# Mamba block and soft decision tree on one core: tail weights scaled in two parts, path matrices and statistics moved, warming products left out

## What is computed

```python
mod = silu(c) @ wmod                            # sa, ca, ga, sb, cb, gb
ga, gb = (2 * (g >= 0) - 1) * maximum(abs(g), 0.25)      # for both gates
h = layernorm(x) * (1 + ca) + sa
xp, z = split(h @ W_in)                         # 256 channels each
u = silu(causal_conv4(xp) + conv_b)
dt_r, B, C = split(u @ W_xp)                    # 8, 16, 16
delta = softplus(dt_r @ W_dt + dt_bias)
for t: s = exp(delta_t * A) * s + delta_t * B_t * u_t     # state 256 x 16
       y_t = s . C_t + D_skip * u_t
x = x + ga * ((y * silu(z)) @ W_out)
h = layernorm(x) * (1 + cb) + sb
gate = sigmoid((h @ Wq.T) @ routers.T)          # 255 nodes of a tree
prob = product of gate or 1 - gate along each of 256 paths
x = x + gb * ((prob @ leaf_values) @ Wo.T + Wo_b)
```

## Time and profile before

| | us |
|---|---|
| median of 3 runs | 511.05 |
| lowest, highest run | 510.07, 511.46 |
| profiled execution, its own time | 512.9 |
| its span, first to last instruction | 510.9 |
| busy: DVE, POOL, PE, ACT | 460.8, 427.0, 407.7, 368.4 |

### The profile page before, as it was taken

How to read it: one execution, slowest core, us unless ns; L and a number is a source line. 1 busy time by engine, 2 the same in 40 slices (tenths; PEclk the granted TensorE clock), 3 DMA queues, 4 the chain that set the end, 5 groups by cost and what they waited for, 6 DMA issues and landing times. The chain is left out here.

```text
span 510.9 us, 6652 instructions
## 1 busy us (share of the span) xinstructions
PE 407.7 (80%) x2111; PEld 283.5 (55%) x2143; DVE 460.8 (90%) x550; ACT 368.4 (72%) x673; POOL 427.0 (84%) x238
## 2 busy tenths in 40 slices
PE   8979652797679967997979787996789786666787
PEld 5437331575556745584647555673547554554554
DVE  5889694899999999999999999998899989999961
ACT  2378972378876998588967998698766896448654
POOL 2549788999999889998899899989799889989700
PEclk9999885799779988898989988999889997796999
DMA  7484033220262008300453008300722027300001
GB/s 176 135 276 163 1 105 147 103 83 1 89 268 83 1 6 308 125 23 1 147 208 104 1 25 330 104 2 0 261 95 103 1 65 291 103 2 1 21 1 41
DMA packets 23714, 51.06 MB, mean 100 GB/s; under 512 B 4473, under 2 KB 13824, under 8 KB 19584
## 3 DMA queue, kind: packets, MB, share of 16 engines
q1 hardware_dynamic: 23680, 50.64, 28.9%
HBM read 48.01 MB, written 2.62 MB: 99 GB/s over the span
## 5 line engine op out<-in xcount | busy, mean ns | idle before, releaser
L568 POOL TENSOR_TENSOR hc<-h,c_rows 128x1024 f32<-128x1024 f32 x126 | 296.0, 2363 | 30.8 <-DVE h L1291 24.0
L1291 DVE TENSOR_TENSOR_SCAN h<-dA,state,dbu 128x512 f32<-128x512 f32 x192 | 233.4, 1264 | 3.8 <-ACT dA L656 3.8
L656 ACT ACTIVATE dA<-delta,a_neg 128x512 f32<-128x512 f32 x256 | 173.9, 686 | 55.7 <-DVE h L1291 54.9
L1070 PE MATMUL yb<-ident,hc 128*128 128x128 f32 x1024 | 162.4, 295 | 26.6 <-POOL hc L568 24.2
L1070 PEld LDWEIGHTS yb<-ident,hc 128*128 128x128 f32 x1024 | 136.9, 154 | 77.4 <-issue 49.3
L1304 DVE TENSOR_TENSOR dbu<-du,bb 128x1024 f32<-128x1024 f32 x88 | 105.5, 1199 | 7.6 <-PE bb L1095 2.6
L555 POOL TENSOR_TENSOR dbu<-du,b_rows 128x1024 f32<-128x1024 f32 x40 | 94.5, 2363 | 4.3 <-DMA b_rows<-bc_dram 4.3
L1291 DVE TENSOR_TENSOR_SCAN h<-dA,dbu 128x512 f32<-128x512 f32 x64 | 74.1, 1204 | 10.0 <-POOL dbu L555 6.6
L1095 PE MATMUL bb<-b_parts,sel 128*128 128x512 bf16 x63 | 27.3, 433 | 45.1 <-DVE dbu L1304 44.3
L976 PE MATMUL mf<-f_hT,w_conv 128*128 128x512 f32 x112 | 53.4, 601 | 1.8 <-ACT zu L715 1.2
L1095 PEld LDWEIGHTS bb<-b_parts,sel 128*128 128x128 bf16 x88 | 9.0, 102 | 63.3 <-DVE dbu L1304 34.5
(11 more groups left out here) (200 smaller groups left out, 529.1 us busy)
## 6 DMA issues: line engine op xcount, KB each, us to landing
c_rows<-bc_dram SPq DMA_DIRECT2D x32, 1024.0 KB, 7.4
b_rows<-bc_dram SPq DMA_DIRECT2D x40, 256.0 KB, 9.0
xs<-in_L_attn_x_dram SPq DMA_DIRECT2D x8, 256.0 KB, 3.8
out_dram<-xs SPq DMA_DIRECT2D x7, 256.0 KB, 5.8
ygT<-in_L_attn_conv_w_dram SPq DMA_DIRECT2D x1, 512.0 KB, 5.0
bc_dram<-xd SPq DMA_DIRECT2D x8, 64.0 KB, 1.6
probT<-in_L_wmod_dram SPq DMA_DIRECT2D x1, 384.0 KB, 3.9
w_in<-in_L_attn_W_in_dram SPq DMA_DIRECT2D x1, 256.0 KB, 4.1
```

Source lines behind the costliest of these rows:

```text
L568: nc.gpsimd.tensor_tensor(hc[:, pair % RC, :, :], h[:, pair % RH, :, :], c_rows[:, q, n % NQ, :].unsqueeze(1).broadcast_to([P, HALVES, T]) ...
L656: nc.scalar.activation(dA[ke % RD][:, :], delta[:, ge % 2, half, :], ACT.Exp, scale=a_neg[:, half, n:n + 1]).then_inc(s_dA, 1)
L1070: last = nc.tensor.matmul(bank[:, tile], hc[:, pair % RC, half, tile], ident[:, :], start=False, stop=n == N - 1, is_transpose=True, skip_ ...
L1291: v.tensor_tensor_scan(h[:, pair % RH, half, :], dA[k % RD][:, :], dbu[:, pair % RW, half, :], start, ALU.mult, ALU.add).then_inc(s_scan, 1)
```

## The change

- **Path matrices.** `make_paths` moves from step 20 of group 0 into POOL's prologue, in three pieces: levels 1 and 2 behind the constants, 3 and 4 behind DVE's normalised x of group 0, 5 to 7 behind the selectors. Each of the three selects of `sel` is cut in two of 1024 columns.
- **Tail weights.** `scale_output_weights` stays at step 20 of group 0; `scale_leaf_weights` runs at step 10 of group 1 and has a semaphore of its own, on which the leaf product of group 0 waits (in group 2).
- **Statistics.** Those of groups 2 and 3 run in DVE's prologue, behind the high and the middle part of B. 1/std and offsets of both groups are made together at steps 2 and 3 of group 0. In the loop, step 19 of group g has the statistics of group g+4, so groups 0 to 3 have one each and group 4 none. The arrays have a place for each group.
- **Gate values.** DVE computes them behind the copy of the dt product weights, no longer ahead of it.
- **Warming.** `keep_warm_on(dA[2], 6)` goes.
- **silu of z.** Step 10 of group g takes z of group g, and runs in group 7 too, with its two table loads.

```diff
-    W_TURN, W_COPY, W_MUL, W_TAKE, W_SCALE = (3, 7), (5, 9), 10, 12, 20
+    NORMS = {2: (4, 3)}
+    NORMS.update({g: (g + 1, g) for g in range(4, GROUPS)})
+    W_TURN, W_COPY, W_MUL, W_TAKE, W_SCALE = (3, 7), (5, 9), 10, 12, (20, 10)
...
+            chain(nc.gpsimd.memset(path[:, :, :], 0.0))
+            chain(nc.gpsimd.memset(path[0:1, 1, :], 1.0))
+            make_paths(1, 3)
+            pool.wait_ge(s_fxh, 1)
+            make_paths(3, 5)
+            pool.wait_ge(s_wconv, TAPS)
...
+            chain(nc.gpsimd.memset(sel[:, :, :], 0.0))
+            for first in (B_HI, B_MID, B_LO):
+                for part in range(2):
+                    some = sel[:, part * N // 2:(part + 1) * N // 2, :]
+                    picked = nc.gpsimd.affine_select(out=some, in_=some, compare_op=ALU.not_equal, fill=1.0,
+                                                     base=-first - part * N // 2, pattern=[[-1, N // 2], [0, P]],
+                                                     channel_multiplier=1)
...
+            make_paths(5, DEPTH)
...
+            def scale_output_weights():
+
                 pool.wait_ge(s_gates, 1)
                 pool.wait_ge(s_w, 16 * n_rest)
...
+            def scale_leaf_weights():
+
+                pool.wait_ge(s_wtake, 1)
...
-                    if g == 0 and s == W_SCALE:
-                        scale_tail_weights()
-                        make_paths()
-                    if 2 <= m2 < GROUPS and s == N_OFF:
-                        offset(m2, f_mv, s_frs, f_nm, s_fnm)
+                    if g == 0 and s == W_SCALE[0]:
+                        scale_output_weights()
+                    if g == 1 and s == W_SCALE[1]:
+                        scale_leaf_weights()
+                    if m2 in NORMS and s == N_OFF:
+                        f_offset(m2, *NORMS[m2])
...
-                        for fz in (0, 1) if f == 1 else (f,):
-                            wait_read(act, "f", "z", 1, fz)
-                            z_part = zu[:, fz % 2, 0:HALVES, :]
-                            nc.scalar.activation(z_part, z_part, ACT.Silu).then_inc(s_zsilu, 1)
+                        wait_read(act, "f", "z", 1, g)
+                        z_part = zu[:, g % 2, 0:HALVES, :]
+                        nc.scalar.activation(z_part, z_part, ACT.Silu).then_inc(s_zsilu, 1)
...
                 gate_products()
-                keep_warm_on(dA[2], 6)
                 pe.wait_ge(s_h0, 1)
...
                         wait_read(pe, "t", "lp", 1, g)
+                        if g == 0:
+                            pe.wait_ge(s_lready, 1)
...
                 gates()
-
                 dve.wait_ge(s_wdtp, 1)
                 v.tensor_copy(w_xdt[:, :, :],
                               dA[0][:, 0:HALVES * DI].rearrange("p (h e) -> p h e", h=HALVES)).then_inc(s_wdt, 1)
+                gate_values()
...
                 v.tensor_copy(b_parts[:, 0, :], mb["f"][0][:, :]).then_inc(s_hi, 1)
+                dve.wait_ge(s_x, 16 * (GROUPS - 2))
+                stats(2, f_bn, f_mv[:, 2, :, :], s_fvar)
                 dve.wait_ge(s_r1, 1)
                 v.tensor_copy(b_parts[B_MID:P, 0, :], mb["f"][0][B_MID:P, :]).then_inc(s_mid, 1)
+                stats(3, f_bn, f_mv[:, 3, :, :], s_fvar)
                 dve.wait_ge(s_r2, 1)
...
-                    if 2 <= g + 3 < GROUPS and s == N_STATS:
-
-                        dve.wait_ge(s_x, 16 * (GROUPS - 2))
-                        if g >= 0:
-                            dve.wait_ge(s_fnm, g + 1)
-                        stats(g + 3, f_bn, f_mv, s_fvar)
+                    if 4 <= g + 4 < GROUPS and s == N_STATS:
+                        stats(g + 4, f_bn, f_mv[:, g + 4, :, :], s_fvar)
```

More of the change, by code:

```diff
@@ L477, in _, with t_offset, f_offset, make_paths @@
             nc.gpsimd.memset(zeros[:, :], 0.0).then_inc(s_const, 1)
[L479 to L503 removed]
+            def t_offset(g):
+                pool.wait_ge(s_trs, g + 1)
+                nc.gpsimd.tensor_tensor(t_nm[:, :], t_mv[:, :, 0], t_nm[:, :], ALU.mult).then_inc(s_tnm, 1)
+            def f_offset(first, end, ready):
+                pool.wait_ge(s_frs, ready)
+                nc.gpsimd.tensor_tensor(f_nm[:, first:end, :], f_mv[:, first:end, :, 0], f_nm[:, first:end, :],
+                                        ALU.mult).then_inc(s_fnm, 1)
+            def make_paths(first, end):
+                for level in range(first, end):
                     nodes = 1 << (level - 1)
@@ new lines, in _ @@
+            chain(nc.gpsimd.memset(sel[:, :, :], 0.0))
[5 more added lines that the diff above has]
+                                                     channel_multiplier=1)
+                    if first == B_LO and part:
+                        picked.then_inc(s_sel, 1)
+                    else:
+                        chain(picked)
@@ L527, in scale_tail_weights @@
+            def scale_leaf_weights():
+                pool.wait_ge(s_wtake, 1)
+                for i in range(2):
+                    chain(nc.gpsimd.tensor_tensor(leaf_out[:, i, :], leaf_out[:, i, :], wo_b[:, :], ALU.add))
+                for b in range(BATCH):
+                    for i in range(2):
                         last = nc.gpsimd.tensor_tensor(leaf_out_g[:, b, i, :], leaf_out[:, i, :], gate_raw[:, b, 1, :],
                                                        ALU.mult)
-                last.then_inc(s_wready, 1)
+                last.then_inc(s_lready, 1)
@@ L586, in chain, with rstd @@
                 act.wait_ge(s_aseq, seq)
-            def rstd(g, mv, rs, nm, ready, done):
-                act.wait_ge(ready, g + 1)
-                chain(nc.scalar.activation(rs[:, :], mv[:, :, 1], ACT.Ln, bias=eps_col[:, :]))
-                chain(nc.scalar.activation(rs[:, :], rs[:, :], ACT.Exp, scale=-0.5))
-                nc.scalar.activation(nm[:, :], rs[:, :], ACT.Copy, scale=-1.0).then_inc(done, 1)
+            def rstd(var, rs, nm, ready, count, done):
+                act.wait_ge(ready, count)
+                chain(nc.scalar.activation(rs, var, ACT.Ln, bias=eps_col[:, :]))
+                chain(nc.scalar.activation(rs, rs, ACT.Exp, scale=-0.5))
+                nc.scalar.activation(nm, rs, ACT.Copy, scale=-1.0).then_inc(done, 1)
             def normalise(g, rs, nm, ready, count, xhat, done):
@@ L1187, in stats @@
             def stats(g, bn, mv, ready):
+                if g:
+                    dve.wait_ge(ready, g)
                 for i in range(TILES):
@@ L1219, in gates, with gate_values @@
                 copy.then_inc(s_gatec, 1)
+            def gate_values():
                 dve.wait_ge(s_gatec, 1)
```

70 lines of the change are left out of this document (27 added, 43 removed).

## The result

| | before | changed |
|---|---|---|
| median of 4 runs each | 511.25 us | 499.09 us |
| lowest, highest run | 510.07, 514.30 | 496.99, 500.31 |
| ratio of the medians, 95% interval | | 0.9755 [0.9717, 0.9793] |
| profiled execution, its span | 512.9, 510.9 | 496.99, 494.8 |
| mean granted clock of PE in it | 0.903 | 0.934 |

The kernel is 12.2 us faster; 498.6 (496.0 to 502.6) was forecast. The profiled execution of the changed kernel is the fastest of its four and that of before was over its median, so the two traces lie 16.1 us apart, 4 more than the medians.

A forecast was written before the change was run, and what follows sets the result against it. DVE, busy 460.8 of 510.9 us, was taken as the bound. Gains of 9.1 + 1.2 + 1.0 + 1.2 = 12.5 us gave 500.4 us for the profiled execution and 498.6 us at the median, range 496.0 to 502.6.

The forecast's parts named there:

- POOL's stop, 9.1 us: Step 20 of group 0: shortening POOL's late work removes DVE's waits of 6.62 and 2.46 us, gain 9.1 us.
- 1.7 costs nothing: Step 20 of group 0: POOL's remaining stop of 1.7 us is under the 2.7 us that buffers absorb, cost 0.
- 2.8 costs nothing: Step 10 of group 1: POOL's new work of 2.8 us is covered by slack, cost 0, bounds 0 and 2.8.
- The rival in which it comes back: Groups 0 and 1: POOL's stops return, 503.1 in full, 500.9 by half; shared chance 0.25 with port and slow clock.
- silu of z, 1.0 us: Step 10 of group 0: one z piece fewer ahead of dA gains 1.0 us; group 7's extra work is covered.
- Warming products, 1.2 us: Prologue, PE: without the filler u products start 2.35 us sooner and end 1.2 us sooner; bounds -1.25 and 2.35.
- if the clock rises at the moment it does now: Prologue, PE: clock rises at 13.9 us, 2.6 of eight records done by then, end at 16.3 instead of 17.5.
- The rival "slower": Into group 0: without the filler the clock stays at 1.2 GHz, PE becomes the bound, 515 and above; chance 0.02.
- The relay behind it: Prologue to first scan: PE's 1.2 us pass on; moving group 2's statistics books nothing more, bounds 0 to 1.2.
- DVE as the prologue's bound: Prologue rival: POOL's selects delay DVE, first part of B 0.9 us later, 500.7; shared chance 0.25 with stops and clock.
- Statistics of group 7, 1.2 us: Group 4 of the loop: DVE has one set of statistics fewer, gain 1.2 us as DVE sets the pace.
- the slack that I forecast from the idle DMA engines: Prologue: x is loaded by 22.4 us, when DMA engines go idle, and DVE reaches the statistics at about 23.6.

The follow-up runs named there:

- e7: Changed kernel with silu of z taken a group ahead again (two pieces at step 10 of group 0, none in group 7): 502.29 us.
- e2: Kernel before without the six warming products, nothing else: 511.68 us, ratio 1.0009 [0.9984, 1.0034].
- e3: Changed kernel with the six warming products back: 498.99 us, ratio 0.9757.
- e6: Changed kernel with statistics where they stood before (group 2's before the first dbu, group g+3's at step 19 of group g): 499.14 us.
- e11: Changed kernel with statistics of group g+3 at step 19 from group 1 on, none in group 0: 498.49 us.
- e12: Changed kernel with selectors made by three whole selects and statistics of group g+3 at step 19 from group 1 on: 498.28 us, ratio 0.9721.
- e9: Changed kernel with leaf weights also scaled at step 20 of group 0, paths still in the prologue: 502.51 us.
- e10: Changed kernel with selectors made by three whole selects of 2048 columns: 498.03 us, ratio 0.9704.
- e1: Kernel before with POOL's part alone (paths in the prologue, selectors halved, tail weights in two parts): 502.19 us, ratio 0.9811.
- e8: Changed kernel with group 4's statistics at step 12 of group 0, groups 5 to 7's at step 19 of groups 2 to 4: 500.27 us.

## Why the prediction came out right

*POOL's stop, 9.1 us.* Right, in size and in mechanism: 8.8 us alone in the runs, both waits gone. The 2.7 us of absorbed stop, read from one row pair, was the number on which "1.7 costs nothing" and "2.8 costs nothing" rested, and stops of three lengths bear it out at 2.4 to 2.7. The rival in which it comes back falls: the buffers absorbed the short stops with DVE running on. One sum of it was off without harm: the last six selects are longer than the mean of 0.49 us of all 14 (3.61 us in the loop and 4.06 in the prologue, not 2.9), and the six half selectors took 7.73 us, not 6.35; so the paths were made at 25.8 us and not at 23.4.

*silu of z, 1.0 us.* Right: 2.81 - 1.86 = 0.95 us between the two kernels, 0.94 in e7, and group 7's hole is covered.

*Warming products, 1.2 us.* Right in direction and mechanism, low in size. The `u` products ended 6.03 us after the start of the gate products instead of 7.84: 1.8 us sooner, where 1.2 were booked within bounds of -1.25 and 2.35. The step that missed is "if the clock rises at the moment it does now", 13.9 us, 4.2 behind the start of the gate products. In the changed kernel's profile the `u` records stand 0.85 and 0.72 us apart at first and 0.43 from 13.22 us on, 3.3 behind that start, so the rise came some 0.9 us sooner. As this moment differs between profiles of the same instructions, the size met here is in part luck. In the runs the gain is not shown: e2's interval allows 0.8 us at most, and e3 equals the changed kernel. The rule of the Trainium skill, "TensorE: Matmul & The Clock Gate", Part 1, that activity itself releases the throttle, agrees with the `u` products: 4.32 us for eight records without the filler, where all at the lower level, 0.85 apart, would have been some 6.8. The rival "slower" falls too: the mean granted clock is 0.934, against 0.903 before.

*The relay behind it.* I booked 0 for the statistics taken out ahead of the first `dbu`, with 0 to 1.2 as bounds, since PE's chain sets the second mark. That was right. The statistics are worth 1.15 us at the first scan (e6), and nothing at the second mark, which follows the end of the `u` records by 25.3 us whether they are moved or not (7.84 and 33.19 before, 6.94 and 32.27 in e3, 6.03 and 31.36 in the changed kernel). The whole 1.8 us at the second mark is the gain of the `u` products.

*DVE as the prologue's bound.* Half true. DVE does run without a gap from 13.51 to the first cast, and there DVE and PE arrive together: PE's product ends at 20.49 + 2.06 = 22.55 and the cast starts at 22.62. In e6 the `u` products end 0.7 us sooner than in the changed kernel, and the first cast still comes 12.7 us after the gate products in both, so there DVE is the bound: a faster PE gains no more at this cast. The two-input operations, which I took as free of POOL, took 1.58 and 1.46 us instead of 0.68 and 0.69. In the changed kernel's profile this costs at most the 0.07 us between 22.55 and 22.62.

*Statistics of group 7, 1.2 us.* **This step failed.** The prediction says that DVE's loop has one fewer, "as DVE sets the pace there". It sets the pace on average, but not at step 19 of group 4: two scans on stands a wait for ACT's `dA`, 0.46 us with the statistics ahead of it and 1.63 without. Group 4 takes 55.34 us instead of 55.51, where 1.2 less was forecast, and e6 has the same time with all statistics at their old places. What is worked off just ahead of a wait is free, and taking it out gained next to nothing. The row with the 0.46 was in the trace of before, in the sum of 7.0 us over 7 waits for `dA`, of which I looked at one only.

So the sum of 12.5 met the measured 12.2 with one term 1.2 too high, one 0.6 too low, and the rest within a few tenths: the terms that traces and runs bear out are 8.8 + 0.95 + 1.8 = 11.6. That the sum came so close is in part luck. The remaining half microsecond is under what the runs can tell. In the two profiles groups 1 to 3 are also 0.3 to 0.5 us shorter each, 1.3 us in all, and the cause stays open. In group 3, 0.41 of the 0.52 us is a wait of DVE for `bb` at 225.87, which the changed kernel's profile lacks. e6, e11 and e12, with the statistics of group g+3 at step 19 as before, have this wait as well, but e7, e9 and e10 have the new steps and a group 3 of 55.8 to 56.0 us, as long as before.

*The low clock.* The two profiles differ by 16.1 us, 4 more than the medians. Before, PE's granted clock is 0.78 and 0.79 from 56 to 64 us, and DVE waits 1.22 us at 62.07 for `bb`; at 363.09 and 365.75 in group 5 it waits 0.57 and 1.44. The changed kernel's profile has nothing at the first two places and 0.42 at the third; its group 5 is 1.3 us shorter. So 1.2 + 1.3 = 2.5 us of the 4 are these. The other profiles speak for episodes and against an effect of the change. A pair of waits for PE, 0.3 to 1.4 and then 1.45 us, stands between 37 and 46 us in those of e1, e2, e6, e7, e9 and e12 and in none of the other eight, with filler and without, with either place of the statistics and of z; e8 and e10 have one in group 2.

## What to carry to other kernels

A stop of an engine that feeds the bottleneck costs its length less what the buffers hold, here 2.4 to 2.7 us: cut such work into pieces under that, or move it to where the feeder idles, and the waits vanish as a whole, as they did here. Before booking the removal of work on the bottleneck engine, look for its next wait: what stands within a few instructions ahead of one can already be free. Where single edits are worth a microsecond and runs spread over four, read them from marks in the trace, measured from a common event, and check the clock of the stretch first.

## What the hardware showed that I had not expected

**The clock falls in one run and not in the next, at the same instructions.** Behind a gap of 1.2 to 2.0 us in PE's work, the products that follow ran in stretches with a granted clock of 0.50 to 0.86 in some profiles and at 1.00 in others with the same or a longer gap (1.44 us at the `u` products of group 1 and 1.99 at 177.06, both in the changed kernel). One such stretch makes DVE wait 1.2 to 2 us for PE, and is of the size of each small term of this change. The rise at the start moves as well: the same six warming products took 1.80, 2.28 and 2.70 us. What decides either, no run here shows.

**Whether a select of POOL holds up a two-input operation of DVE depends on when it runs.** `scalar_tensor_tensor` over 512 columns took 0.68 us alone, 1.58 and 1.46 while a selector of 1024 columns was being made (1.1 to 1.35 us per select), and 0.72 and 0.69 beside the small path selects. The Trainium skill, "SBUF — State Buffer", section "Who interferes with whom", has an operation of DVE with two SBUF inputs contend with an instruction of GpSimd that reads SBUF, and calls the shared ports an exclusive lock. The delays of 0.90 and 0.77 us, each under the length of one select, agree. In the other direction little shows: the last six path selects took 4.06 us in the prologue and 3.61 in the loop, 0.1 us more for each, and whether DVE is the cause no run shows.

**DVE can now outrun the loads.** Statistics of group 2 at about 23 us wait for x in some profiles (0.34, 0.35, 0.66, 1.00 and 1.38 us) and not in others (0 in the changed kernel's): the slack that I forecast from the idle DMA engines, DVE at 23.6 against 22.4, is about nil.
